# A state-space block's sequence stage: Softplus in one function, straight-line code instead of engine loops, and deeper rings for the products with C

## The reference

```
xf, res = split(x @ in_proj.T);  xf = silu(conv(xf));  xb = silu(conv(xf, w_b))
for direction 0 (on xf) and direction 1 (on xb, reversed in time):
  delta, B, C = split(u @ x_proj.T);  dt = softplus(delta @ dt_proj.T + bias)   # 512 channels
  for n in 0..15:  state = exp(dt * A_n) * state + dt * u * B_n                 # a scan over 512 positions
                   y    += state * C_n      (with a guard factor, see below)
  y = (y + u * D) * silu(res)
x = layernorm(x + (y_0 + y_1) @ out_proj.T)
slots = softmax-weighted sums of layernorm(x);  16 experts: gelu(slots Wg) * (slots Wu) @ Wd
x = layernorm(x + combine @ experts)
```

## Time and profile before

| | us |
|---|---|
| median of three runs | 6184.25 |
| the profiled execution, device time | 6181.29 |
| its span in the trace | 6179.4 |
| sequence stage, up to the expert stage's first matmul | 5198.0 |
| first merge load | 5868.5 |

### The profile page before, as it was taken

How to read it: one execution, slowest core, us unless ns; L and a number is a source line. 1 busy time by engine, 2 the same in 40 slices (tenths; PEclk the granted TensorE clock), 3 DMA queues, 4 the chain that set the end, 5 groups by cost and what they waited for, 6 DMA issues and landing times. The chain is left out here.

```text
span 6179.4 us, 71038 instructions
## 1 busy us (share of the span) xinstructions
PE 5160.9 (84%) x14632; PEld 2583.4 (42%) x14632; DVE 4752.2 (77%) x4180; ACT 4356.5 (71%) x6761; POOL 4787.8 (77%) x2264
## 2 busy tenths in 40 slices
PE   6888888888888888888888888888888887999977
PEld 2333333333333343433333333333333344555566
DVE  5898988888989898989888888888888881222233
ACT  4888888888888888888888888888888873111100
POOL 4999999999999999999999999999999980000000
PEclk9999999999999999999999999999899998999988
DMA  2444444434443444444444444443434332233265
GB/s 73 127 124 126 123 126 122 125 121 129 121 129 121 129 121 128 122 124 124 123 125 125 122 124 123 126 123 121 126 123 125 122 115 75 84 99 99 64 229 204
DMA packets 555713, 755.58 MB, mean 122 GB/s; under 512 B 124059, under 2 KB 272411, under 8 KB 553245
## 3 DMA queue, kind: packets, MB, share of 16 engines
q1 hardware_dynamic: 555293, 752.04, 40.1%
HBM read 662.04 MB, written 89.82 MB: 122 GB/s over the span
## 5 line engine op out<-in xcount | busy, mean ns | idle before, releaser
L1022 DVE TENSOR_TENSOR_SCAN e_ps<-e_ps,g_ring 128x1024 f32<-128x1024 f32 x1024 | 2346.0, 2291 | 252.2 <-ACT e_ps L824 222.2
L654 POOL TENSOR_TENSOR g_ring<-dtu,b_ring 128x1024 f32<-128x1024 f32 x1026 | 2482.0, 2427 | 49.1 <-DVE e_ps L1022 30.2
L1187 PE MATMUL y_ps<-v_ring,ident 128*128 128x512 f32 x3080 | 1683.3, 659 | 428.6 <-POOL v_ring L663 275.9
L663 POOL TENSOR_TENSOR v_ring<-z_ring,c_ring 128x1024 f32<-128x1024 f32 x768 | 1844.8, 2403 | 147.6 <-PE y_ps L1187 147.4
L824 ACT ACTIVATE e_ps<-dt,a_neg 128x512 f32<-128x512 f32 x2050 | 1397.1, 681 | 539.6 <-DVE z_ring L1035 306.6
L834 ACT ACTIVATE f_ring<-rsum,consts,a_neg_half 128x512 f32<-128x512 f32 x2050 | 1646.4, 803 | 0.9
L1187 PEld LDWEIGHTS y_ps<-v_ring,ident 128*128 128x128 f32 x3080 | 595.2, 209 | 1206.2 <-issue 586.6
L1035 DVE SCALAR_TENSOR_TENSOR z_ring<-f_ring,e_ps 128x1024 f32<-128x1024 f32 x768 | 934.6, 1217 | 103.0 <-DVE e_ps L1022 96.2
L1187 PE MATMUL y_ps<-v_own,ident 128*128 128x512 f32 x1028 | 541.3, 620 | 0.0
L1120 PE MATMUL side<-u,conv_diag 128*128 128x512 f32 x1088 | 490.6, 594 | 26.5 <-ACT disp_ring L785 25.1
L1297 ACT ACTIVATE x_act<-x_gate,x_bg 128x512 f32<-128x512 f32 x128 | 87.9, 687 | 562.6 <-PE x_gate L1329 562.6
(11 more groups left out here) (141 smaller groups left out, 5885.5 us busy)
## 6 DMA issues: line engine op xcount, KB each, us to landing
b_ring<-bc_scr SPq DMA_DIRECT2D x1027, 256.0 KB, 3.5
c_ring<-bc_scr SPq DMA_DIRECT2D x1025, 256.0 KB, 3.4
pT_scr<-rowT_ring SPq DMA_DIRECT2D x136, 256.0 KB, 3.7
m_pT<-pT_scr SPq DMA_DIRECT2D x16, 2048.0 KB, 8.6
sT_scr<-sT_ring SPq DMA_DIRECT2D x272, 64.0 KB, 2.8
x_xT<-sT_scr SPq DMA_DIRECT2D x16, 1024.0 KB, 8.9
eo_scr<-x_eo SPq DMA_DIRECT2D x32, 512.0 KB, 5.1
m_eo<-eo_scr SPq DMA_DIRECT2D x16, 1024.0 KB, 11.2
```

The costliest lines, as they stand in the source:

```text
L654: pool.tensor_tensor(g_ring[:, k], dtu[d][:], both(b_ring[:, k:k + 1]), ALU.mult).then_inc(g_done, 1)
L663: pool.tensor_tensor(v_ring[:, k], z_ring[:, k], both(c_ring[:, k:k + 1]), ALU.mult).then_inc(v_pool, 1)
L1022: dve.tensor_tensor_scan(e, e, g, 0.0, ALU.mult, ALU.add).then_inc(scan_done, 1)
L1187: pe.matmul(y_ps[:, t % 2], ident[:], v, start=(t % (TILES // PAIRS) < 2), stop=True, skip_group_check=True).then_inc(v_used, 1)
```

## The change

1. **Softplus.** ACT computes it with one function, chunk by chunk, from the two banks into `dt`, both at lag 2 of the pair's second slot. Abs, Exp, e+1, (e+1)-1 and Ln on ACT, the addition on DVE and the two subtractions on POOL are gone. POOL's product with u comes at `DTU_LAG` = 4, the running sum at lag 4, the cut at lag 7. A bank of a dt slot is held 2 tiles, not 5.
2. **No engine loops.** Every `Fori` of the three stages becomes a Python `range`: straight-line code, constants in place of registers. SP's `go` is gone.
3. **Rings.** `v_ring` has six slots and `v_own` four, used in turn by the products that each engine makes.
4. **Lags.** `Y_LAG` and `GATE_TILE` go from 6 to 10. The anchors of what follows go back by four tiles as well: the output projection from tile 8 to 12, the LayerNorm's steps from 15..25 to 19..29, the transposes xnT from 27 to 31; dt0_2 goes from 34 to 36; dt1_2 (66) and all later anchors stay. The D products (`SKIPS`) of the second pair go from tiles 72..75 to 76..79. SP's load of the next x goes from step 17 to 19.

```diff
-HOLD = {..., "dt0": 5, "dt1": 5, ...}
+HOLD = {..., "dt0": 2, "dt1": 2, ...}
-STATS_TILE, VAR_TILE, ROUGH_TILE, RSTD_TILE, APPLY_TILE = 15, 18, 20, 22, 25
-EARLIEST = {("dt1", 0): 1, ("out", 0): 8, ("xnT", 0): APPLY_TILE + 2, ("dt0", 2): 34, ("dt1", 2): 66, ("in0", 2): 79,
+STATS_TILE, VAR_TILE, ROUGH_TILE, RSTD_TILE, APPLY_TILE = 19, 22, 24, 26, 29
+EARLIEST = {("dt1", 0): 1, ("out", 0): 12, ("xnT", 0): APPLY_TILE + 2, ("dt0", 2): 36, ("dt1", 2): 66, ("in0", 2): 79,
             ("dt0", 0): 97, ("slots", 7): 122}
...
-    Y_LAG = 6
-    GATE_TILE = 6
+    VR = 6
+    Y_LAG = 10
+    GATE_TILE = 10
-    SP_LAG, X_STEP = 4, 17
+    SP_LAG, X_STEP = 4, 19
-    FIX_LAG, DT_LAG, RSUM_LAG, CUT_LAG = 6, 8, 10, 12
+    DTU_LAG, RSUM_LAG, CUT_LAG = 4, 4, 7
...
+    def same_slot_before(i):
+        if on_dve(i):
+            return max(j for j in range(i - STEPS, i) if on_dve(j) and dve_steps(j) % 4 == dve_steps(i) % 4)
+        return max(j for j in range(i - STEPS, i) if not on_dve(j) and pool_steps(j) % VR == pool_steps(i) % VR)
+
+    def v_slot(i):
+        return v_own[:, dve_steps(i) % 4] if on_dve(i) else v_ring[:, pool_steps(i) % VR]
...
-        v_ring = sb("v_ring", [P, 3, 2, L])
-        v_own = sb("v_own", [P, 2, 2, L])
+        v_ring = sb("v_ring", [P, VR, 2, L])
+        v_own = sb("v_own", [P, 4, 2, L])
...
             # gpsimd
-            def softplus_fix(at, s): ...
-            def softplus_end(at, s): ...
+            def dtu_of_pair(at, s):
+                d, i = int(TABLE[s][0][-1]), TABLE[s][1]
                 for j in (s - 1, s):
                     pool.wait_ge(side_free[at.bank(j)], at.freed(j))
                 pool.tensor_tensor(dtu[d][:], dt[d][:], u[d][:, i - 1:i + 1, PAD:], ALU.mult).then_inc(dtu_done, 1)
...
-                pool.wait_ge(v_used, b * TILES + (2 * (last_on_pool(before(i)) + 1) + CR))
-                pool.tensor_tensor(v_ring[:, k], z_ring[:, k], both(c_ring[:, k:k + 1]), ALU.mult).then_inc(v_pool, 1)
+                pool.wait_ge(v_used, b * TILES + (2 * (same_slot_before(i) + 1) + CR))
+                pool.tensor_tensor(v_slot(i), z_ring[:, k], both(c_ring[:, k:k + 1]), ALU.mult).then_inc(v_pool, 1)
...
             # scalar, side_step at lag 2
-                    elif kind in ("dt0", "dt1"):
-                        act.activation(sp_exp[d][:, i % 2], src, ACT.Abs).then_inc(abs_done, 1)
+                    elif kind in ("dt0", "dt1") and i % 2 == 1:
+                        act.activation(dt[d][:, 0], side[:, at.bank(s - 1)], ACT.Softplus).then_inc(
+                            side_free[at.bank(s - 1)], 1)
+                        act.activation(dt[d][:, 1], src, ACT.Softplus).then_inc(free, 1)
-                if kind in ("dt0", "dt1"):      # lags 3 to 6: Exp, Identity, Identity, Ln
...
             # vector, side_step
-                    if lag == 4:
-                        dve.wait_ge(exp_done, at.chunk(s))
-                        dve.scalar_tensor_tensor(out=dt[d][:, i % 2], in0=src, scalar=0.0, in1=sp_exp[d][:, i % 2],
-                                                 op0=ALU.max, op1=ALU.add).then_inc(free, 1)
                     if lag == RSUM_LAG and i % 2 == 1:
-                        dve.wait_ge(dt_done, at.pair(s))
+                        for j in (s - 1, s):
+                            dve.wait_ge(side_free[at.bank(j)], at.freed(j))
...
             # every engine, every stage; the same for the other bounds and stages
-            with dve.Fori(0, B, 1) as b:
+            for b in range(0, B, 1):
```

More of the change, by code:

```diff
@@ L284, in sequence_stage @@
         a_neg_half = sb("a_neg_half", [P, NDIR, KI, N])
-        consts = sb("consts", [P, 5])
-        guard_bias, one, cut, less_one = (consts[:, k:k + 1] for k in (0, 1, 2, 4))
+        consts = sb("consts", [P, 4])
+        guard_bias, one, cut = (consts[:, k:k + 1] for k in range(3))
         ident = sb("ident", [P, P])
@@ L682, in _ @@
                 inputs(0, gi)
-            with pool.Fori(0, B, 1) as b:
+            for b in range(0, B, 1):
                 at = At("loop", b, pool)
@@ L843, in _ @@
                 guard(0, 0, h)
-            with act.Fori(0, B, 1) as b:
+            for b in range(0, B, 1):
                 at = At("loop", b, act)
@@ L868, in _ @@
             dve.memset(cut, CUT)
-            dve.memset(less_one, -1.0)
             dve.memset(border[:, 0:L - 1], 1.0)
@@ L1192, in _ @@
                 fill(pro, s)
-            with pe.Fori(0, B, 1) as b:
+            for b in range(0, B, 1):
                 at = At("loop", b, pe)
@@ L1276, in _ @@
             load(0, 0)
-            with sp.Fori(0, E - 2, 2) as e:
+            for e in range(0, E - 2, 2):
                 load(e + 1, 1)
@@ L1289, in _ @@
         def _(act):
-            with act.Fori(0, E // 2, 1) as e2:
+            for e2 in range(0, E // 2, 1):
                 for q in range(2):
@@ L1303, in _ @@
             dve.sem_inc(eo_done, RT)
-            with dve.Fori(0, E // 2, 1) as e2:
+            for e2 in range(0, E // 2, 1):
                 for q in range(2):
@@ L1320, in _ @@
         def _(pe):
-            with pe.Fori(0, E // 2, 1) as e2:
+            for e2 in range(0, E // 2, 1):
                 for q in range(2):
@@ L1394, in _ @@
             if B > 2:
-                with sp.Fori(0, B - 2, 2) as b:
+                for b in range(0, B - 2, 2):
                     load(b + 1, 1)
@@ L1410, in _ @@
             dve.sem_inc(y_done, 2 * LT)
-            with dve.Fori(0, B // 2, 1) as b2:
+            for b2 in range(0, B // 2, 1):
                 for q in range(2):
@@ L1434, in _ @@
         def _(pe):
-            with pe.Fori(0, B // 2, 1) as b2:
+            for b2 in range(0, B // 2, 1):
                 for q in range(2):
```

83 lines of the change are left out of this document (18 added, 65 removed).

## The result

| | us | ratio to before | 95% interval |
|---|---|---|---|
| before (4 runs beside it) | 6184.03 | | |
| after, median of 4 (6014.98 to 6041.35) | 6023.36 | 0.9747 | 0.9733 to 0.9761 |
| forecast | 5950 (5790 to 6095) | 0.962 | |

The kernel is 2.5% faster; the forecast was 3.8%. The profiled execution of after took 6041.35 us, span 6039.5, the longest of the four, so what is counted in its trace (the long sequences above all) is counted in the slowest of them. They are set against each other by their ratios to before; 0.001 is 6.18 us.

A forecast was written before the change was run, and what follows sets the result against it. The prediction took the DVE and ACT loop as the bound, POOL a close second. Terms of -13.7 us a sequence gave 216 us, plus 16 outside the sequence loop: 232 off 6181.3, about 5950 us, range 5790 to 6095.

The forecast's parts named there:

- loop edges: Sequence loop: DVE's 3.00 us idle at each jump back goes, 15 edges at -3.0 us, bounds 0 and -3.0.
- merge stage: Merge rounds: SP's straight-line issue of loads saves 1.0 us in 7 rounds, with the edges 8 us (0 to 20).
- addition: DVE's 8 additions of max(s, 0) a sequence go: -3.6 us a sequence (-2.4 to -5.4).
- crowding: ACT's Identities before the burst go: -3.0 of DVE's 14.4 us waits for ACT a sequence (0 to -6).
- issue: The running sum's wait put down to issue goes with the long chain ahead of it: -0.9 us a sequence.
- prologue: Ahead of the first scan: the first pair's shorter Softplus chain saves 8 us (4 to 10).
- rings: Rings and lags: most of DVE's column product and gate waits go, -4.2 us a sequence (0 to -4.2).
- squeeze: Output projection to dt1_2: work of 39 tiles has 35, costing +1.0 us a sequence (0 to +9.7).
- (a): Rival: POOL decides, so its removed work and waits shorten each sequence to 283.1 us: 5728 us, chance 0.12.
- (c): Rival: the four lost tiles before dt1_2 are paid in full, 139 us given back: 6089 us, chance 0.13.
- (b): Rival: Softplus shares a table with Exp and Tanh, so both loads go, 125 us more: 5825 us, chance 0.08.
- (d): Rival: a long Softplus on ACT, 3.0 us a call, adds 310 us: 6260 us, chance 0.04.

The follow-up runs named there:

- e1: The kernel before with straight-line code in all three stages and without the signal ahead of SP's DMAs, nothing else changed: 6170.01 us, ratio 0.9973.
- e2: e1 plus the one-function Softplus with its lags, but rings of three and two and PE six tiles behind as before: 6092.39 us, ratio 0.9854.
- e5: The kernel before with straight-line code, new rings, lags and anchors, old Softplus kept but without POOL's two subtractions of each pair: 6163.86 us, ratio 0.9958.
- e7: The changed kernel with POOL's product with u made three times instead of once for each pair: 6061.49 us, ratio 0.9797.
- e9: The changed kernel with DVE's addition of max(s, 0) put back at lag 3: 6082.38 us, ratio 0.9838.
- e6: The changed kernel with Exp in place of Softplus, so the two table loads round each pair go: 5950.19 us, ratio 0.9608.
- e12: e5 without ACT's two Identities of each pair as well: 6129.78 us, ratio 0.9913.
- e8: The changed kernel with the running sum at lag 6 instead of 4 and the cut at 9 instead of 7: 6117.31 us, ratio 0.9882.
- e10: The changed kernel with POOL waiting for one running sum a sequence, that of the first pair of direction 1: 5991.30 us, ratio 0.9692.
- e4: The changed kernel with POOL waiting for every running sum of DVE before its next g product: 6054.05 us, ratio 0.9785.
- e11: The changed kernel with the running sum at lag 3 instead of 4: 5963.40 us, ratio 0.9649.

## Why the forecast was right in direction and 1.3% too fast

By groups, the forecast against what the ratios give:

| part | forecast | measured |
|---|---|---|
| loop edges 45 and merge stage 8 | -53 | -17 (e1) |
| Softplus: addition 58, crowding 48, issue 14, prologue 8 | -128 | -74 (e2 to e1) |
| rings 67, squeeze +16 | -51 | -66 (after to e2) |
| all | -232 | -156 |

The split between the last two parts hangs on the order: with the rings first they measure -10, and Softplus -130, about what was forecast for it.

- **What bounds the kernel** (DVE and ACT, not POOL): right in the main. Taking POOL's work away gives nothing on balance (e5), putting 302 us of it back costs 31 (e7), and POOL waits for DVE's scan in after, while DVE waits for POOL once, at the first scan. Rival (a) falls. But POOL is not free of weight: it holds up DVE's running sum.
- **Loop edges, -45**: wrong in size. The gap of the earlier trace rows is gone, but as e1 shows 12 sequences got 3.0 us at the edges and some 5.6 us each of shorter latency behind scan and guard, and gave nearly all back in waits for rows of C, ACT and PE. The bound of 0 that the prediction gave the edges was the right end. The 6.0 us that "stay" in the reading of the earlier trace rows did not stay; they went with the loops and registers.
- **DVE's addition, -58**: +56 when put back one tile behind the Softplus (e9), by another mechanism.
- **POOL's subtractions, 0**: 0 (e5), as a balance of 59 us less idle time and 62 us more of running sums.
- **Rings and lags, with the squeeze, -51**: -66, but only beside the short Softplus; alone -10. The means were not those of the text: the column product's wait stayed (3.1 us), and what went was the wait of POOL for PE and of DVE at the gate. Rival (c), the squeeze in full, falls by the sum; the squeeze alone was not tried. Its condition was read too high: the 86.3 us of PE belong to 104 us and 42 tiles, so that the 39 tiles hold about 80 us, less than the 85 in which they were to pass.
- **Softplus**: 0.60 and 0.59 us against 0.58, burst 3.69 us against 3.7. Rivals (b) and (d) fall by the timeline. The Trainium skill, "ScalarE: Activation LUTs", Table sets: the hidden batching unit, says that each set has one expensive function as its anchor; it names Tanh in the set of Exp and does not list Softplus. The trace agrees that it is in another set, with 65 loads to Softplus and 65 back at 1.28 us. Dropping both was worth 86 us (e6), where (b) had 125.
- **Crowding, -48**: the two Identities alone 28 (e12), in its bounds; DVE's waits for the decay fell by 49, and longer running sums took back 28.
- **The running sum** is the step that failed: the prediction kept its length and its place free of cost, and only took away its wait for issue. Its lag went from 10 to 4, next to the burst and beside POOL's product with u. That did two things. It put the sum where DVE would have waited for ACT, worth 83 us against two tiles later (e8), which was not forecast; and it let the first sum wait for three POOL products in 11 of 16 sequences, +77 us of DVE's busy time, worth 34 net (e10).
- **Prologue, -8**: DVE's first scan came at 105.21 us, not 102.89, so +2.3 (103.1 to 105.5 in e4, e7, e8, e10 and e11, which have the same prologue). That scan still waited for POOL's first product, 10.44 us there against 4.63. POOL itself was free at 97.07 us, not at some 100.5 as before, but began that product only at 102.75, and SP issued the first loads of rows of B at 99.42 us instead of 96.05. So the trace points at those rows and not at the Softplus; no run tested it.
- **Merge, -8**: from the first load to the end 310.9 us before (5868.51 to 6179.4, rows 10) and 309.3 after (5730.23 to 6039.5): -1.6. What holds its rounds beside SP's issue was not tried.

One way to lay out the shortfall of 76 us is: loops and merge 36, prologue 10, the long first sum 34, less 15 that the rings gave beyond their term; 65 of 76. This is bookkeeping and not proof: the terms were measured beside different kernels, the split between Softplus and rings hangs on the order, and the 20 us by which the crowding fell short and the unforecast gain of the sum's place are not in it. The remaining 11 stay unassigned; the runs of after alone lie 26 us apart. That the total landed in the range owes something to such errors of both signs.

## What to carry to other kernels

When the profile shows an engine at 96% but its waits name a slower one, and nobody waits for it, do not count its removed work as time gained; here the two ratios were 0.9958 and 0.9957. But look at what its instructions meet once they have moved: here they lengthened a neighbour's by 62 us. Side work has a price by its place: put what a late engine doesn't hold up into the moment in which you wait for that engine, here the running sum directly behind the function that needs its own table (one tile earlier: 61 us, part of them by missing POOL's products; two tiles later: 83 us lost). And a latency removed from every step (loop edges, register waits) pays only up to the next operand, so look for what would be late next, here rows of C, before multiplying it out.

## What the runs showed of the hardware

- DVE's running sum and POOL's products, with two SBUF operands each, took turns: a sum ended 2.14 to 2.15 us after the last POOL product of usual length (49 of 49 in after), and alone took 2.3 (e4). A waiting sum did not always get the next turn: it took 3.28 us (POOL's next product 4.34), or 9.85 us while three of POOL's took 2.33, 2.17 and 2.34. In one sequence or the next the same program fell into either. DVE's scan of the state, in place in PSUM with one SBUF operand, took 2.27 to 2.30 us throughout, with POOL at work beside it.
- Straight-line code with constants in place of registers shortened the step from a scan's start to its guard product's from 2.48 to 2.38 us, and from guard to DVE's own product from 1.44 to 1.26 (medians of before, e1 and after; e1 changes nothing else but the `go` signals). The loop and the registers were not tried apart.
- A Softplus costs what other functions cost (0.59 to 0.60 us for 128x512), but had 1.28 us of table load on either side.
